# Layer 1's linear attention on pairs of token tiles, with one running-sum product for two tiles

## The reference, cut to what matters

```python
q, k = elu(x @ Wq[l] + bq[l]) + 1, elu(x @ Wk[l] + bk[l]) + 1      # v = x @ Wv[l] + bv[l]
scores = where(tril, einsum('bnchd,bnkhd->bnhck', q, k), 0)        # within a chunk of 128
intra, den_intra = scores @ v, scores.sum(-1)
inter, den_inter = q @ KVcum, q @ Kcum                             # from all chunks before
out = (inter + intra) / (den_inter + den_intra + 1e-6)
x = x + out @ Wo[l] + bo[l];  x = _ln(x);  x = _ln(x + gelu(x @ W1[l] + b1[l]) @ W2[l] + b2[l])
```

## Time and profile before

| | |
|---|---|
| time, median of 3 runs | 1735.81 us (1734.9 to 1736.24) |
| span of the profiled execution | 1734.0 us, 31744 instructions |
| the profiled execution's own time | not listed apart; the runs' times lie 0.9 to 2.2 us above its span |
| PE busy | 1698.0 us (98%) |
| DVE busy | 1234.6 us (71%) |
| POOL busy | 1218.5 us (70%) |
| ACT busy | 1088.9 us (63%) |
| PE weight loads | 1300.6 us (75%) |

### The profile page before, as it was taken

The page is one execution under the profiler, slowest core; times in us unless marked ns, Lnnn a source line. Parts: engine busy times, 40 slices in busy tenths (PEclk is TensorE's granted clock), DMA queues, the critical chain, the costliest instruction groups (busy, mean ns, idle before and its releaser), DMA issues.

```text
span 1734.0 us, 31744 instructions
## 1 busy us (share of the span) xinstructions
PE 1698.0 (98%) x10006; PEld 1300.6 (75%) x10006; DVE 1234.6 (71%) x4490; ACT 1088.9 (63%) x2904; POOL 1218.5 (70%) x1771
## 2 busy tenths in 40 slices
PE   8999999999999999999999999999999899999998
PEld 5788888876667676676666677767788787788976
DVE  7864335688987988988899866445566766578773
ACT  6555226556677678777776786446546666665656
POOL 5655649898878987888789785135347876666667
PEclk9999999999999999999999999999999999999999
DMA  7100000010000000000000000000000001000002
GB/s 254 71 29 1 1 2 3 3 51 1 1 1 1 1 1 1 1 1 1 1 1 1 1 11 6 1 1 7 2 3 3 1 18 31 21 1 2 2 2 73
DMA packets 24027, 26.70 MB, mean 15 GB/s; under 512 B 3492, under 2 KB 20772, under 8 KB 23476
## 3 DMA queue, kind: packets, MB, share of 16 engines
q1 hardware_dynamic: 23860, 24.67, 4.4%
HBM read 22.52 MB, written 2.15 MB: 14 GB/s over the span
## 4 chain that ended last, share of the span: by engine, by line
PE 80%; POOL 6%; DVE 6%; ACT 4%; issue 2%; DMA 0%; SPq 0%; POOLq 0%; ACTq 0%; DVEq 0%
PE ps L87 74%; PE ps L90 7%; POOL arena L104 6%; ACT arena L98 4%; DVE arena L104 2%; DVE arena L110 1%; DVE arena L130 1%; DVE arena L147 1%; ACT arena L99 0%; DVE arena L133 0%; ACT L98 0%; DVE arena L107 0%; DMA arena<-in_x 0%; DVE arena L136 0%; DVE ps L147 0%
## 5 line engine op out<-in xcount | busy, mean ns | idle before, releaser
L104 POOL TENSOR_TENSOR arena<-arena 128x512 f32<-128x512 f32 (+6 forms) x836 | 715.5, 869 | 278.4 <-DVE arena L110 96.9
L98 ACT ACTIVATE arena<-ps 128x128 f32<-128x128 f32 (+11 forms) x1204 | 338.6, 326 | 394.1 <-PE ps L87 287.8
L87 PE MATMUL ps<-arena 128*128 128x128 f32 (+4 forms) x2792 | 441.0, 291 | 10.0 <-DVE arena L104 3.5
L87 PEld LDWEIGHTS ps<-arena 128*128 128x128 f32 x2792 | 373.3, 191 | 97.9 <-issue 46.5
L104 DVE TENSOR_TENSOR arena<-ps,arena 128x128 f32<-128x128 f32 (+4 forms) x696 | 312.9, 468 | 176.0 <-PE ps L87 163.6
L98 ACT ACTIVATE arena<-arena 128x128 f32<-128x128 f32 (+1 forms) x836 | 321.2, 439 | 51.3 <-POOL arena L104 39.6
L87 PE MATMUL ps<-arena,moe 128*128 128x256 f32 (+1 forms) x960 | 288.2, 439 | 0.0
L87 PE MATMUL ps<-arena,cst 128*128 128x504 f32 (+2 forms) x768 | 283.6, 489 | 2.2 <-ACT arena L98 1.1
L98 ACT ACTIVATE arena<-ps,cols 128x512 f32<-128x512 f32 x324 | 216.8, 688 | 103.3 <-PE ps L87 96.5
L104 POOL TENSOR_TENSOR arena<-arena,cst 128x144 f32<-128x144 f32 (+7 forms) x536 | 186.2, 356 | 93.0 <-ACT arena L98 57.4
L110 DVE SCALAR_TENSOR_TENSOR arena<-ps,arena 128x128 f32<-128x128 f32 (+1 forms) x476 | 156.6, 364 | 120.4 <-PE ps L87 94.2
(11 more groups left out here) (120 smaller groups left out, 1756.5 us busy)
## 6 DMA issues: line engine op xcount, KB each, us to landing
rows<-in_rows SPq DMA_DIRECT2D x1, 2253.0 KB, 14.2
arena<-in_x SPq DMA_DIRECT2D x8, 256.0 KB, 5.3
wf<-in_wf SPq DMA_DIRECT2D x2, 1024.0 KB, 6.6
arena<-in_L_ffn_W SPq DMA_DIRECT2D x8, 256.0 KB, 2.9
out_dram<-arena SPq DMA_DIRECT2D x8, 256.0 KB, 2.7
wmod<-in_wmod SPq DMA_DIRECT2D x4, 384.0 KB, 7.7
arena<-kept SPq DMA_DIRECT2D x24, 64.0 KB, 2.9
arena<-kept SPq DMA_DIRECT2D x8, 192.0 KB, 3.0
```

Of the source, the lines that this page charges most:

```text
L87: return UNSENT if self.e is None else self.e.matmul(out, lhsT, rhs, start=start, stop=stop)
L98: return self.e.activation(out, in_, func, bias=bias, scale=scale)
L104: return UNSENT if self.e is None else self.e.tensor_tensor(out, a, c, op)
```

## The change

Tiles 2T and 2T+1 are now worked on together as pair T (4 pairs instead of 8 tiles), and the tokens of a pair are interleaved: row i of side s holds token 2i+s of the pair's 256. The running sum over rows then runs over both sides at once.

- Entering and leaving the stage, SP moves each element from the normal order to the interleaved one (`queue_pairs`, into `m.xs`) and back (`queue_unpaired`, into `m.hT`): 8 transfers of 64 KB each way, for each element, each waited for.
- POOL forms the products of k and v in two parts of the values e: u = 0 (values 0 to 3) and u = 1 (values 4 to 7; ACT's copy of k is the ninth), each for both sides (1024 elements). The two parts share one buffer, so u = 1 waits for the reduction of u = 0 (`kv_free`).
- New: DVE adds the two sides (512 and 640 elements, all in SBUF), and PE multiplies only the sum by the triangle: 512, then 256 and 384 columns.
- The sums are multiplied by q of each side (DVE 2x512 and 2x384 out of PSUM, POOL 2x256), then reduced (1024 to 128 and 1280 to 160 elements).
- The even token of a row has seen its odd neighbour too much. New: DVE multiplies q of side 0 by k of side 1 (128), reduces with a minus sign (16), multiplies by v of side 1 (144), and adds that to the result (144). All inputs are in SBUF.
- State, inter part, turning, Wo, reciprocal and residual are done once for a pair: `l1s` as two products into one sum, `l1i`, `l1q`, `l1a` and `l1w` as two products into one bank, the element-wise steps at twice the width.
- The room of an element grows by 30 columns (`REST`), and all four strings of `TURNS` are new.

The core of the diff (turns, marks and the ACT part left out):

```diff
+        kv = r.take(1280)
+        self.kvs = [kv[:, 0:1024].rearrange("p (n c) -> p n c", c=32), kv.rearrange("p (n c) -> p n c", c=40)]
+        self.att = kv[:, 0:256]
...
-        PARTS = ((13, 16), (0, 7), (7, 13))
+        PARTS = (((0, 4),), ((3, 5), (0, 3)))
...
+                    for u in range(2):
+                        for e0, e1 in PARTS[u]:
+                            yield
+                            ps = banks.take(pe, b, b, "l1p", l, T, u, e0)
+                            pe.wait_ge(*at("l1sum", b, l, T, u))
+                            pe.mm(of_head(ps[:, 0:(e1 - e0) * 128], 8 * (e1 - e0)), tri,
+                                  m.kvs[u][:, 0:16, 8 * e0:8 * e1]).then_inc(*pe.up(b, "l1p", b, l, T, u, e0))
...
+                    dve.tt(prod, m.q(0), m.k(1), ALU.mult).then_inc(*dve.up(b))
+                    dve.reduce(gain, of_head(prod, 8), negate=True).then_inc(*dve.up(b))
+                    dve.tt(of_head(own, 9), gain.unsqueeze(2).broadcast_to([128, 16, 9]), of_head(m.v(1), 9),
+                           ALU.mult).then_inc(*dve.up(b, "l1c", b, l, T))
...
+                        dve.tt(kv[:, 0:16, :], kv[:, 0:16, :], kv[:, 16:32, :], ALU.add).then_inc(
+                            *dve.up(b, "l1sum", b, l, T, u))
+                        for s in range(2):
+                            dve.wait_ge(*at("l1p", b, l, T, u, e0))
+                            dve.tt(m.part(u, s, e0, e1), of_part(ps[:, 0:128 * (e1 - e0)], e1 - e0),
+                                   by_e(m.q(s), e1 - e0), ALU.mult)
+                        dve.reduce(of_head(m.nd, 9)[:, :, 4 * u:4 + 5 * u],
+                                   kv.rearrange("p n (e d) -> p n e d", d=8)).then_inc(*dve.up(b, "l1r", b, l, T, u))
+                    dve.tt(m.nd[:, 0:144], m.nd[:, 0:144], own, ALU.add).then_inc(*dve.up(b))
...
+                    for u in range(2):
+                        kv_free(pool, b, l, T, u)
+                        pool.tt(m.kvs[u][:, :, 0:32].rearrange("p n (e d) -> p n e d", d=8), by_e(m.k(), 4),
+                                of_head(m.va, 9)[:, :, 4 * u:4 * u + 4].unsqueeze(3).broadcast_to([128, 32, 4, 8]),
+                                ALU.mult).then_inc(*pool.up(b, "l1o", b, l, T, u))
...
+        def interleave(name, b, h, dst, src):
+            for side in range(2):
+                for s in range(2):
+                    load(name, dst[64 * side:64 * side + 64, 4 * h + s:4 * h + 4:2, :],
+                         src[s:128:2, 4 * h + side:4 * h + 4:2, :])
```

More of the change, by code:

```diff
@@ L391 @@
 TURNS = {
[L392 to L425, removed]
@@ new lines, in l1_dve @@
+                    yield
+                    dve.wait_ge(*dve.last(b))
+                    dve.reciprocal(m.rec[:, 32:64], m.rec[:, 0:32]).then_inc(*dve.up(b))
+                    yield
+                    dve.wait_ge(*dve.last(b))
+                    dve.tt(of_head(m.att, 8), top, m.rec[:, 32:64].unsqueeze(2).broadcast_to([128, 32, 8]),
+                           ALU.mult).then_inc(*dve.up(b, "l1att", b, l, T, free=(b, "l1i", l, T) if T else None))
+                    if T < NT // 2 - 1:
+                        for s in range(2):
+                            yield
+                            feature_dve(b, m, l, T + 1, s)
@@ new lines, in l1_dve @@
+                    yield
+                    ps = banks.get(b, "l1w", l, T)
+                    dve.wait_ge(*at("l1w", b, l, T))
+                    dve.wait_ge(*at("l1res", b, l, 0, T // 2))
+                    x2 = m.xs[:, 256 * T:256 * T + 256]
+                    dve.tt(x2, ps[:, 0:256], x2, ALU.add).then_inc(*dve.up(b, free=(b, "l1w", l, T)))
+                    yield
+                    dve.wait_ge(*dve.last(b))
+                    yield from stats(b, [(m.tile(t), t) for t in (2 * T, 2 * T + 1)])
@@ L1724, in l1_dve @@
+                    yield
+                    if T % 2:
+                        yield from scales(b, "l1stats", b, l, 1, T // 2, t0=2 * T - 2, t1=2 * T + 2)
                 yield
@@ L1817, in l1_pool @@
                 pool.wait_ge(*at("l1n_act", b, "out", h))
-                pool.tt(v, v, over(r.row(1)), ALU.mult).then_inc(*pool.up(b))
-                pool.wait_ge(*pool.last(b))
+                pool.tt(v, v, over(r.row(1)), ALU.mult).then_inc(*pool.up(b, "l1paired", b, h))
+                yield
+            for h in range(2):
                 xg = r.x[:, 4 * h:4 * h + 4, :]
-                pool.tt(xg, xg, v, ALU.add).then_inc(*pool.up(b, "l1x_out", b, h))
+                pool.wait_ge(*arrives(f"unpaired{b}_{h}", 4))
+                pool.tt(xg, xg, four(m.hT[:, 512 * h:512 * h + 512]), ALU.add).then_inc(*pool.up(b, "l1x_out", b, h))
                 yield
```

587 lines of the change are left out of this document (316 added, 271 removed).

## The result

| | before | after |
|---|---|---|
| median of the runs, us | 1736.03 (1734.9 to 1737.82) | 1915.59 (1908.18 to 1919.46) |
| ratio to before, 95% interval | 1 | 1.1026 [1.0999, 1.1052] |
| span of the profiled execution, us | 1734.0 | 1916.0 |
| forecast, us | | 1775 (1690 to 1850) |

A forecast was written before the change was run, and what follows sets the result against it. PE and DVE were taken as nearly balanced in layer 1, with DVE setting the middle after the change. Stretches summed to 1736 us, 2 more than before; 39 us of DVE waits for POOL gave 1775 (range 1690 to 1850).

The forecast's parts named there:

- The wait that is new: Layer 1, middle stretch: two-SBUF-input DVE instructions stand still until a running POOL instruction ends; 260 x 0.15 = 39 us.
- the sum of 1736: Whole kernel, five stretches added without waits of DVE for POOL: 2 us more than before, 1736 us.
- the upper bound of 0.42: Mean wait per two-SBUF-input DVE instruction with POOL in such an instruction 60% of the time, mean rest 0.7 us.
- DVE's work: Layer 1's attention: 10.8 us a pair on DVE instead of 9.2, 102 us more over 64 pairs.
- The edges: Stretches outside the middle: 28 us less before the first start, then 34 more, 4 less and 1 more.
- PE: -133 us: Layer 1 on PE: 123 us of triangle columns, about 8 of products and 2 of transposes saved.
- POOL at nothing: POOL loses about 20 us of work in layer 1; having room in the middle stretch, this counts as nothing.
- Spread: Rival: new turns level DVE's idle time over layer 1's window, below 900 us; 1694 us in all; 25%.
- Hidden waits: Rival: DVE 99% busy in the middle, waits for POOL only 0.04 us each; 1727 us; 10%.
- Lock: Rival: DVE's two-SBUF-input instructions wait 0.42 us each for POOL, 109 us in all; 1845 us; 20%.
- The chain: Rival: shared buffer makes a pair wait for POOL, DVE, PE, DVE twice; 16 us a pair; inside range, no chance given.
- the signs that I named: PE well below 98%, DVE 94% or more in a middle of at least 600 us, 512-element sums' median above 0.69 us.

The follow-up runs named there:

- the kernel with one SBUF input: Changed kernel with all 336 two-SBUF-input DVE instructions of layer 1's attention made one-input reductions, second operand left out: 1779.38 us, ratio 1.0257.
- the kernel without new DVE steps: Changed kernel with DVE's sums, product, its reduction, correction and last addition left out, PE multiplying side 0 alone: 1757.75 us, ratio 1.0124.
- the filler: Kernel before plus five unused DVE instructions per two tiles of layer 1's attention: 1905.71 us reading one SBUF input, 1988.78 us reading two.
- half the triangle: Kernel before with half the columns of every PE triangle product left out: 1720.29 us, ratio 0.991.

## Why the prediction was wrong

The step that failed is the price of the new wait: 39 us in the forecast, 136 in the runs. A second term was too small by 42 us, the stretches outside the middle. Step by step; the kernel with one SBUF input is the forecast's case without waits, so it can be laid beside the sum of 1736.

| stretch | forecast without waits | one input | after |
|---|---|---|---|
| before the first start | 230 | 254 | 257 |
| first to fourth element | 148 | 170 | 182 |
| middle | 628 | 595 | 713 |
| to the end of layer 1 | 192 | 196 | 200 |
| rest | 538 | 563 | 564 |
| sum | 1736 | 1778 | 1916 |

The forecast's fourth and fifth rows rest on the cut at 1197; by the cut at 1187, which the measured columns have, they are 182 and 548.

- **The wait that is new: the step that failed.** 39 us were forecast (0.15 us on each of 260), 136 were measured by taking it away; by the trace it is 0.37 us on each of 336, hard under the upper bound of 0.42. The mechanism, the place and the bounds were right, the value was not. I took it near the groups' means of the earlier trace rows, and a part of those instructions lies in stretches where POOL is busy 50 and 59% (37.82 of 75 us from 100 us on, 64.44 of 110 from 1000 us on), not 84% as in the middle. I also argued that DVE's work follows directly on POOL's, so that POOL had just ended. The timeline at 862.56 and 865.96 shows it in the midst of an instruction; that this is another element's multiplication is likely with four elements in turn, but I have not followed it. The price to take here was share of time x mean rest of POOL's instruction, the upper bound. Two smaller slips: 336 such instructions and not 320, and nothing was booked for those outside the middle, which holds 118 of the 138 us. The rule of the Trainium skill (SBUF - State Buffer, section "Who interferes with whom"), that the interface is held for a whole instruction, would have given 1845 with my sum: nearer by 70 us. The trace agrees with it in the two instructions that end 0.17 and 0.55 us behind POOL's.
- **DVE's work: right.** Forecast +102 us; with one input DVE's busy time is 1331.0 for 1234.6, +96. That it is 96% busy in the middle was right too (571.78 of 595); only 603 us of its work were forecast to fall there.
- **The edges: too low by 75 us, and the middle too high by 33; 42 in all.** I priced an element's worth of work at PE's full pace (106 + 42, 71, 41). In the new order PE stands still in places where it never did: 24.5 us of the first 257 and 18.8 of the next 182, for 6.8 and 0.1. 11.8 us are the entry's transfers (taken away in the kernel without new DVE steps), which I booked at 0. There was no cover: without them the first start comes 6.6 us earlier (248.9 for 255.5) and the next stretch is 5 us shorter. The 12 "without cover" stood for entering and leaving together; what leaving costs no run shows. The rest of the head's 46 us and the 29 us of the last two rows are put down to the new order and its work, with the transfers on leaving as an untested rival; that split is only argued.
- **PE: -133 us, of which the record shows little.** With one input PE is busy 63.5 us less, after 24.6. The columns did go; the busy time of the others grew (last section). It cost the forecast nothing, since PE no longer set the middle.
- **POOL at nothing: right.** With one input POOL has 11.5 us less busy time than before (forecast 20), after it has 26.7 more. A part of that is the lock the other way round (last section), and halving POOL's products gave 8 us.
- **The rivals.** Spread (1694) is refuted: the window from layer 1's first to last instruction is 1095 us, and 961 with one input, not under 900. Hidden waits (1727) as well. Lock (1845) had nearly the right price, 109 for 136, on a sum 43 us too low: 1736 + 43 + 136 = 1915. The chain, left inside the range, may have a part: with the new DVE steps gone and both PE and POOL lightened the kernel still takes 1739, and which chain holds it is open.

So most of the signs that I named came out (DVE 95% in the middle, PE far below 98%, the middle over 600 us, a long tail on the sums). One did not: the median of the 45 sums of 512 elements that are listed one by one is 0.68 us and not above 0.69, since most of them don't wait and the others wait about 1 us. The value that sets the size, 0.37 for 0.15 us, was the one I had to guess.

## What to carry to other kernels

A DVE instruction with two SBUF inputs beside a GpSimd that multiplies most of the time should be booked at GpSimd's share of time in such instructions times the mean rest of them, and not at what quiet places of the trace show. That product was 0.42 us; one placement measured 0.37, the filler 0.23, so it is an upper estimate; in the filler the later ones of each row paid less than the first. Short ones pay as much as long ones, so they are the first to give another form: one input from PSUM, or a reduction of one input. Here both forms ran without the wait, but that a reduction can do the work of the sums or the correction was not tried. In a kernel of fixed turns, test first what relief of each engine is worth (here 16 of 123 us for PE at 98%), and don't count on an engine's idle time to hide new work: 153 us put on a DVE that was busy 87% cost 170, and 125 us taken from it later gave 22. An order searched anew has waits of its own at the edges: read PE's idle time there, don't carry over its old pace.

## What the runs showed of the hardware

**PE's clock is lower where PE waits.** Before, the granted clock is 0.99 to 1.00 in every stretch. After, two neighbouring slices of the middle:

```profile
850.00:900.00 50.00, 31.94 (x100) 18.96 (x101) 46.26 (x100) 14.63 (x46) 31.41 (x28) 0.73 0.00 0
900.00:950.00 50.00, 40.98 (x205) 27.23 (x204) 49.61 (x125) 31.94 (x71) 36.69 (x33) 1.00 0.00 1
```

0.73 is a mean of the two levels, 2.4 and 1.2 GHz, in a slice in which PE stands still for 18 of 50 us; in the next one it stands still for 9 and the clock is 2.4 GHz throughout. The same group of matmuls in two kernels, after and without the new DVE steps:

```profile
L87 PE MATMUL ps<-arena,cst 128*128 128x512 f32 x128 | 86.9, 773 | 67.5 <-DVE arena L104 67.2 <-ACT arena L98 0.2
```

```profile
L87 PE MATMUL ps<-arena,cst 128*128 128x512 f32 x128 | 67.3, 614 | 7.2 <-POOL arena L104 3.9 <-ACT arena L98 3.3
```

The product that waits for DVE takes 773 ns for 614. By the mean clocks of the middle stretch, 0.91 for 0.97, 614 ns would become about 655 (an estimate); the rest of the difference is open, for the clock at just these matmuls is not known. What the lower clock costs the kernel was not separated.

**PE's busy time is not PE's work.** With the filler, the kernel before computes the same on PE, and PE's busy time rises from 1698.0 to 1758.3 and 1778.7 us, a part of it by the clock (0.94 and 0.91 in the middle). With half the triangle it falls by 68.5 us where 123 us of columns went, at a granted clock of 1.00 in every stretch. The earlier trace rows shows what can be behind that: the record of 504 columns is 1.02 us long and the next one starts 0.86 us after it, so 0.16 us of it lie under the next; where the next one has to wait, they count as busy time. That this is the whole difference no run shows.

**The wait goes both ways.** Near 869 us the sum starts first, and POOL's multiplication takes 2.50 us where its neighbours above take 1.99:

```profile
868.89 0.81 DVE L104 TENSOR_TENSOR arena<-arena 128x640 f32<-128x640 f32 x1
...
869.05 2.50 POOL L104 TENSOR_TENSOR arena<-arena 128x1024 f32<-128x1024 f32 x1 [1.76 <-DVE arena L147]
```

In the mean it is less: the 128 multiplications of 1024 elements take 2047 ns after and 1997 both with one input and without the new DVE steps, 6 us in all. The 37 ns from the 1960 of the kernel before to 1997 are not the lock of these instructions; they stay open.

**Not every DVE instruction with one SBUF input goes free.** The 64 scalings of 128 elements (`TENSOR_SCALAR`, one SBUF input, outside layer 1's attention) take 383 ns in the mean before and 545 after, though the change does not touch them; in the kernel with one input they take 559, so it is not the two-input steps that slow them:

```profile
L107 DVE TENSOR_SCALAR arena<-arena 128x128 f32<-128x128 f32 x64 | 33.0, 545 | 8.8 <-POOL arena L107 5.6 <-issue 1.5 <-POOL arena L104 1.4
```

Single ones take 0.34 us. Four of them from 1345.10 on take 3.38 us, while POOL multiplies from 1345.03 to 1349.57. That it is POOL that holds them is read from this place, not tested; the group is 10 us longer than before.
